# Layer 0's routed experts: slots sorted in one run per array half, weights gathered by indirect loads into six fixed buffers, the shared expert ahead of them

## The chip, the cores and the metric

The kernel runs on one core of a Trainium2 chip. The metric is the device time of one execution in microseconds (us). Before the change, three runs took 3437.78, 3443.05 and 3444.62 us (median 3443.05).

## The reference

A four-layer network on a sequence of 8 x 64 = 512 tokens of width 512 (float32); every layer has a cross attention, a second mixer and a feed-forward, each added to the residual. The change is in the feed-forward of layer 0, a mixture of eight experts of which each token uses two, plus a shared expert that all tokens use:

```python
    def _L0_ffn_ref(x, ln_scale, ln_bias, gate_w, Wg, Wu, Wd, sWg, sWu, sWd):
        ...
        xn = (xf - mu) * jax.lax.rsqrt(var + LN_EPS) * ln_scale + ln_bias
        logits = xn @ gate_w.T
        probs = jax.nn.softmax(logits, axis=-1)
        tk_probs, tk_idx = jax.lax.top_k(probs, TOP_K)
        tk_probs = tk_probs / (jnp.sum(tk_probs, axis=-1, keepdims=True) + EPS)
        ...
        out = _swiglu(xf, sWg, sWu, sWd)
        for e in range(NUM_EXPERTS):
            out = out + w[:, e:e + 1] * _swiglu(xf, Wg[e], Wu[e], Wd[e])
```

with `_swiglu(x, wg, wu, wd) = silu(x @ wg) * (x @ wu) @ wd`. The hidden width of an expert is 1024, so each of its three matrices has 512 x 1024 float32 values, 2 MiB (2.097 MB).

## The kernel before

The kernel is one program for the core's five engines (TensorE, abbreviated PE; VectorE, DVE; ScalarE, ACT; GpSimd, POOL; SyncE, SP), written engine by engine. Each engine runs its own list in order, and semaphores (`wait_ge`, `then_inc`) tie the lists together. A stage ends when all engines have ended their lists for it.

`L0_ffn` first normalises the tokens (`normalise`), then routes. Each expert's tokens are cut into slots of 64 rows; the 1024 token-expert pairs and eight experts need at most 23 slots. Routing runs on VectorE: scores, the two best experts, the rank of each token within its expert (TensorE's `rank`), from that the slot row of each token (`where_to`, ready with the signal `placed`), and the expert of each slot from slot 8 on (`ids`, ready with `ids_ready`). The first slot of expert e is slot e; further slots of crowded experts come behind, from slot 8 on. POOL then scatters the token rows into the table `slot_x` in DRAM (8 indirect transfers, L1764), and reads the slots back by groups (`load`, L1770).

TensorE works on two slots at a time, one per half of its array (64 columns of the 128). Such a group, of which there are 12 (`GROUPS`, the fourth has one slot), runs through: gate and up matmuls (L1863, into four PSUM banks), turning of the next group's tokens (L1836), turning of the hidden rows (L1876), down matmuls (L1888). ACT applies silu and copies results out of PSUM, VectorE multiplies gate and up (L2064). POOL stores the group's output rows into the table `slot_y` (L1781). At the end POOL gathers every token's two rows from `slot_y` (L1786), VectorE adds them weighted (L2082); the last group doesn't go through DRAM but through a matmul with one-hot rows (`hots`, turned at L1895; used at L1901) and an addition (L2087).

The weights come through a ring of eight units of 2 MiB in SBUF, filled by SP in the order of use (`units`): shared up columns 0 to 3, then for each group its gate, up and down matrices; the shared up columns 4 to 7 after the third group (`UP_AFTER`), the shared down matrix after the seventh (`DOWN_AFTER`). The first eight units are sent ahead, during `normalise` (L177): the experts of slots 0 to 7 are known without routing. Each later unit waits for the matmuls that read the unit eight places before it (L1750, L1747); from slot 8 on SP reads the expert's number from `ids`.

The shared expert's up part (`shared_up`, L1827) runs by eight column blocks: the first four during routing, followed by idle matmuls (`run_idle`, L150) until the slots are there, the other four after the third group; its down part (L1911) after the seventh group.

Of the kernel before, what the change touches and what calls it, by code (L numbers as in the profile page):

```python
# [20 lines left out]
LAST_ROWS = SLOT_ROWS - P  # L21
# [1574 lines left out]
def L0_xattn_and_attn(m):  # L1596
# [4 lines left out]
    with m.local(qT=[P, C, N], oT=[P, C, N], w=[P, C, D], bo=[P, D], b=[P, 3, C],  # L1601
# [3 lines left out]
        def clear_slots(pool):  # L1605
            pool.memset(zero[:], 0.0).then_inc(*zeroed.up())
            pool.wait_ge(*zeroed.at(1))
            for p in range(SLOT_ROWS // P):
                pool.dma_start(m.slot_x[p * P:(p + 1) * P, :], zero[:]).then_inc(*filled.up(16))
            pool.dma_start(m.slot_y[LAST_ROWS:SLOT_ROWS, :], zero[:]).then_inc(*filled.up(16))  # L1610

        def slots_cleared(pool):
            pool.wait_ge(*filled.at(SLOT_ROWS // P * 16 + 16))
# [34 lines left out]
def L0_ffn(m):  # L1648
# [9 lines left out]
    s = m.sig  # L1658
    vectors = s("gate_vectors")
    landed = [s(f"unit_landed{r}") for r in range(R)]  # L1660
# [12 lines left out]
    units, read_by = [], []  # L1673
    done = {"Wg": gate_done, "Wu": lift_done, "Wd": down_done}
    halves = [0]
    for p, group in enumerate(GROUPS):
        halves.append(halves[-1] + len(group))
    units.append(("up", 0))
    read_by.append((up_done, 4))
    for p, group in enumerate(GROUPS):  # L1680
        for name in ("Wg", "Wu", "Wd"):
            for slot in group:
                units.append((name, slot))
                read_by.append((done[name], p + 1 if name == "Wd" else halves[p + 1]))
        if p == UP_AFTER:
            units.append(("up", 1))
            read_by.append((up_done, FC))
        if p == DOWN_AFTER:
            units.append(("down", 0))
            read_by.append((shared_done, T))  # L1690
    where = {key: u for u, key in enumerate(units)}
    parts = [2 if name == "up" else 1 for name, _ in units]

    def after(u):
        return 16 * sum(parts[v] for v in range(u % R, u + 1, R))

    with m.local(ring=[P, R, C * F], gw=[P, C, E], gws=[P, 2, C, E], ln=[P, 2, C], before=[P, E, E], place=[P, E]) as \
            (ring, gw, gws, ln, before, place):
        def rows_of(u, k):
            return ring[:, u % R, :].rearrange("p (k f) -> p k f", k=k)  # L1700

        def pairs_of(u):
            name, slot = units[u]
            if name == "up":
                part = ring[:, u % R, :].rearrange("p (two k f) -> p two k f", two=2, k=C)
                cols = slice(HALF * slot, HALF * slot + HALF)
                return [(part[:, i], d[f"L0_ffn_{w}"][E, :, :, cols]) for i, w in enumerate(("Wg", "Wu"))]
            if name == "down":
                return [(rows_of(u, FC), d["L0_ffn_Wd"][E])]
            return [(rows_of(u, FC if name == "Wd" else C), d[f"L0_ffn_{name}"][slot])]  # L1710

        normalise(m, m.y, m.x, 1e-5, dstT=m.yT, ahead=[
            *[(landed[u], *pairs_of(u)) for u in range(1)],
# [3 lines left out]
            *[(landed[u], *pairs_of(u)) for u in range(1, R)]])  # L1717
        vectors_made = vectors.made
        first_landed = [(landed[r].sem, landed[r].made) for r in range(R)]
        with m.local(hs=[P, FC, N], xt=[P, 2, D], xT=[P, 2, C, P], sg=[P, 2, HALF], h=[P, F], hT=[P, FC, P], o=[P, 2, D],  # L1720
                     w=[P, T, E], sc=[P, T, E], sel=[P, T, E], pos=[P, T, E], tmp=[P, T, E], one=[P, T],
                     cmp=[P, T, E, E], eq=[P, T, E, E], tri=[P, P], full=[P, P], nb=[P, 5, E], least=[P, 2, T],
                     share=[P, 2, T], marks=[1, 2 * E], idf=[1, 2 * E], index=[P, P], hots=[P, 2, T, P], hotsT=[P, N],
                     away=[P, 2, T]) as \
                (hs, xt, xT, sg, h, hT, o, w, sc, sel, pos, tmp, one, cmp, eq, tri, full, nb, least, share, marks, idf,
                 index, hots, hotsT, away), \
                m.nc.sbuf_tensor("slot_of_token", [P, 2, T], mybir.dt.uint32) as where_to, \
                m.nc.sbuf_tensor("expert_of_slot", [1, 2 * E], mybir.dt.int32) as ids, \
# [3 lines left out]
            def await_unit(eng, u):  # L1732
                sem, made_before = first_landed[u % R]
                eng.wait_ge(sem, made_before + after(u) - after(u % R))

            @block.sync
            def _(sp):
                for u in range(R, len(units)):
                    name, slot = units[u]
                    signal, n = read_by[u - R]  # L1740
                    sp.wait_ge(*signal.at(n))
                    if name in done and slot >= E:
                        if (name, slot) == ("Wg", E):
                            sp.wait_ge(*ids_ready.at(1))
                        expert = sp.value_load(ids[0:1, slot - E:slot - E + 1], min_val=0, max_val=E)
                        source = d[f"L0_ffn_{name}"][bass.ds(expert, 1)].rearrange("o p k f -> p (o k) f")
                        sp.dma_start(rows_of(u, FC if name == "Wd" else C), source).then_inc(*landed[u % R].up(16))  # L1747
                    else:
                        for dst, source in pairs_of(u):
                            sp.dma_start(dst, source).then_inc(*landed[u % R].up(16))  # L1750

            @block.gpsimd
            def _(pool):
# [13 lines left out]
                pool.wait_ge(*scattered.at(32 * T))  # L1767

                def load(p):
                    pool.dma_start(xt[:, p % 2, :], m.slot_x[p * P:(p + 1) * P, :]).then_inc(*x_landed[p % 2].up(16))  # L1770

                load(0)
                load(1)
                for p in range(len(GROUPS)):
                    if p + 2 <= LAST:
                        pool.wait_ge(*x_turned.at(p + 1))
                        load(p + 2)
                    if p == LAST:
                        break
                    pool.wait_ge(*o_taken.at(p + 1))  # L1780
                    pool.dma_start(m.slot_y[p * P:(p + 1) * P, :], o[:, p % 2, :]).then_inc(*stored[p % 2].up(16))  # L1781
                for i in range(2):
                    pool.wait_ge(*stored[i].at(16 * ((LAST + 1 - i) // 2)))
# [8 lines left out]
            def _(pe):  # L1792
# [25 lines left out]
                def shared_up(n):  # L1818
                    u = where[("up", n // 4)]
                    wb = ring[:, u % R, :].rearrange("p (two k f) -> p two k f", two=2, k=C)  # L1820
                    if n % 4 == 0:
                        await_unit(pe, u)
                    if n >= 2:
                        pe.wait_ge(*hs_ready.at(n - 1))
                    for kind in range(2):
                        for k in range(C):
                            ins = pe.matmul(ps[:, 2 * kind + n % 2, :], wb[:, kind, k, n % 4 * P:(n % 4 + 1) * P],  # L1827
                                            m.yT[:, k, :], start=(k == 0), stop=(k == C - 1))
                    ins.then_inc(*up_done.up())

                def turn_x(p):
                    pe.wait_ge(*x_landed[p % 2].at(16 * (p // 2 + 1)))
# [9 lines left out]
                for n in range(4):  # L1842
                    shared_up(n)
                    if n == 1:
                        rank()
# [2136 lines left out]
```

## Time and profile before

| | |
|---|---|
| three runs | 3437.78, 3443.05, 3444.62 us |
| profiled execution: span from first to last instruction | 3436.7 us |
| profiled execution: time outside the span | not shown by the page; the median of the runs is 6.4 us above the span |
| PE busy | 3113.6 us (91%) |
| DVE, ACT, POOL busy | 1225.3, 710.6, 391.5 us (36, 21, 11%) |
| DMA | 653.75 MB, mean 190 GB/s |
| the stage of the change | about 413 to 838 us of the span |

A busy PE is not PE at its peak; idle time of an engine that isn't the bottleneck costs nothing. A matmul of float32 data shows as two records. Loads are credited to the queue that describes them: the hardware queue (q1) for those issued by SP, the software queue (q0) for those issued by POOL; both use the same 16 DMA engines. A DMA share of 1.00 means that all 16 were busy.

### The profile page before, as it was taken

What the parts mean: (1) busy time and instruction counts of PE and PEld (TensorE: products, weight loads), DVE (VectorE), ACT (ScalarE), POOL (GpSimd) and SP (SyncE); (2) the same over time, 40 slices, a digit from 0 to 9 for tenths busy, and PEclk for the clock granted to TensorE, in tenths of its full rate; (3) what the DMA queues carried; (4) which work ended last, traced back from release to release, by engine and by line L of the source; (5) the groups of instructions that cost most, each with busy time, mean ns of one, the idle gap of its engine ahead of it and who ended that gap; (6) DMA issues with size and microseconds to landing.
All of it is one profiled execution on the core that took longest, in us unless ns stands there. A gap on an engine that the chain in (4) does not pass through costs nothing. (4 is left out here: it accounts for less than half of the span.)

```text
span 3436.7 us, 44844 instructions
## 1 busy us (share of the span) xinstructions
PE 3113.6 (91%) x18245; PEld 1708.9 (50%) x18245; DVE 1225.3 (36%) x2569; ACT 710.6 (21%) x1365; POOL 391.5 (11%) x386
## 2 busy tenths in 40 slices
PE   9998999998999999999899999999999997666666
PEld 6776643434444544444567675446886742111111
DVE  3675520002444569865341223114555220000000
ACT  2443111011333331110112130104442311000000
POOL 4452010001000000001000000005441000000000
PEclk9999999999999999999999999999999999788888
DMA  3112189997111212220641113971103069999998
GB/s 108 46 34 78 74 337 412 419 409 323 74 49 49 77 31 68 98 98 25 236 158 43 52 63 118 421 304 50 37 13 136 29 268 417 420 420 420 420 420 359
DMA packets 104218, 653.75 MB, mean 190 GB/s; under 512 B 20216, under 2 KB 29432, under 8 KB 41208
## 3 DMA queue, kind: packets, MB, share of 16 engines
q1 hardware_dynamic: 99360, 637.67, 46.2%
q0 software_dynamic: 4160, 13.63, 1.0%
q8 instruction: 120, 1.97, 0.2%
q14 instruction: 42, 0.34, 0.0%
q10 hardware_dynamic: 536, 0.14, 0.0%
HBM read 641.89 MB, written 9.50 MB: 190 GB/s over the span
## 5 line engine op out<-in xcount | busy, mean ns | idle before, releaser
L3105 PE MATMUL banks<-ring,h 128*32 128x512 f32 x1024 | 164.9, 750 | 87.0 <-DMA ring<-in_L_ffn_w 62.2
L3088 PE MATMUL banks<-ring,mine 128*32 128x512 f32 x1024 | 165.2, 695 | 54.8 <-DMA ring<-in_L_ffn_w 54.3
L924 PE MATMUL banks<-ring 128*128 128x256 f32 x784 | 179.9, 381 | 0.0
L1863 PE MATMUL banks<-ring,xT 128*64 128x512 f32 x736 | 165.4, 603 | 12.1 <-DMA ring<-in_L_ffn_Wg 6.1
L509 PE MATMUL banks<-normed_features,first 128*128 128x256 f32 x768 | 167.2, 379 | 0.4 <-ACT normed_features L476 0.4
L3216 DVE COPY mine<-mT 128x32 f32<-128x32 f32 x31 | 5.6, 181 | 446.4 <-PE banks L3088 446.4
L924 PEld LDWEIGHTS banks<-ring 128*128 128x128 f32 x784 | 144.5, 190 | 28.7 <-issue 11.4
L509 PEld LDWEIGHTS banks<-normed_features,first 128*128 128x128 f32 x768 | 145.3, 190 | 21.6 <-issue 2.0
L434 POOL TENSOR_TENSOR rstd_pairs<-var_eps_pairs,minus_half 128x4 f32<-128x4 f32 x30 | 30.8, 1028 | 1072.9 <-DVE var_eps_pairs L422 897.5
L3105 PEld LDWEIGHTS banks<-ring,h 128*32 128x32 f32 x1024 | 25.9, 121 | 197.6 <-DMA ring<-in_L_ffn_w 148.5
L1863 PEld LDWEIGHTS banks<-ring,xT 128*64 128x64 f32 x736 | 60.7, 139 | 113.3 <-issue 112.2
L3088 PEld LDWEIGHTS banks<-ring,mine 128*32 128x32 f32 x1024 | 34.5, 117 | 165.1 <-DMA ring<-in_L_ffn_w 112.8
L897 PE MATMUL banks<-big 128*128 128x512 f32 x256 | 115.5, 595 | 0.0
L893 PE MATMUL banks<-big 128*128 128x512 f32 x256 | 113.1, 595 | 1.0 <-ACT big L1067 1.0
L3354 PE MATMUL banks<-big,ring 128*128 128x512 f32 x256 | 111.2, 594 | 0.0
L150 PE MATMUL banks<-identity 128*128 128x128 f32 x740 | 96.4, 290 | 12.7 <-PEq L142 12.7
L150 PEld LDWEIGHTS banks<-identity 128*128 128x128 f32 x740 | 92.2, 204 | 21.1 <-issue 20.8
L1888 PE MATMUL banks<-ring,hT 128*64 128x512 f32 x368 | 89.2, 619 | 14.2 <-DMA ring<-in_L_ffn_Wd 11.7
L2064 DVE TENSOR_TENSOR h<-banks,sg 128x512 f32<-128x512 f32 x23 | 15.9, 692 | 239.4 <-PE banks L1863 214.3
L509 PE MATMUL banks<-normed_features,ring 128*128 128x256 f32 x448 | 97.7, 379 | 0.9 <-DMA bo<-in_L_xattn_bo 0.5
L509 PEld LDWEIGHTS banks<-normed_features,ring 128*128 128x128 f32 x448 | 84.6, 190 | 13.4 <-issue 1.1
L3354 PEld LDWEIGHTS banks<-big,ring 128*128 128x128 f32 x256 | 48.2, 190 | 62.6 <-issue 62.6
(668 smaller groups left out, 5280.7 us busy)
## 6 DMA issues: line engine op xcount, KB each, us to landing
ring<-in_L_ffn_w SPq DMA_DIRECT2D x256, 1024.0 KB, 27.1
ring<-in_L_ffn_Wd SPq DMA_DIRECT2D x24, 2048.0 KB, 21.4
ring<-in_L_ffn_Wg SPq DMA_DIRECT2D x23, 2048.0 KB, 24.7
ring<-in_L_ffn_Wu SPq DMA_DIRECT2D x23, 2048.0 KB, 19.4
wb<-in_L_ffn_W SPq DMA_DIRECT2D x32, 1024.0 KB, 19.3
first<-in_L_ffn_W SPq DMA_DIRECT2D x16, 1024.0 KB, 14.5
second<-in_L_ffn_W SPq DMA_DIRECT2D x12, 1024.0 KB, 18.5
ctxT<-in_ctxT SPq DMA_DIRECT2D x8, 1024.0 KB, 4.9
```

What stands on the lines that cost most here:

```text
L150: pe.matmul(m.ps[:, bank, 0:P], m.ident[:], m.ident[:], start=True, stop=True)
L434: pool.tensor_tensor(m.rstd2[:, 2 * half:2 * half + 2, :].rearrange("p t i -> p (t i)"), m.den2[:, 2 * half:2 * half + 2, :].rearrange("p ...
L509: ins = pe.matmul(m.ps[:, self.banks[q % R], 0:256], w[:, k, mm * P:(mm + 1) * P], m.yT[:, k, 256 * half:256 * half + 256], start=(k == 0) ...
L893: ins = pe.matmul(ps[:, u % 2, :], wkb[:, k, u * P:(u + 1) * P], (extraT if knorm else ctxT[:, par])[:, k, :], start=(k == 0), stop=(k == ...
L897: ins = pe.matmul(ps[:, u % 2, :], ctxT[:, par, k, r * P:(r + 1) * P], wvb[:, k, :], start=(k == 0), stop=(k == C - 1))
L924: ins = pe.matmul(halves(n % 2)[:, r, :], a, x, start=(k == 0), stop=(k == 1))
L1863: ins = pe.matmul(ps[H * side:H * side + H, 2 * kind + half, :], xT[:, p % 2, k, H * own:H * own + H], rows_of(where[(name, slot)], C)[:, ...
L1888: ins = pe.matmul(ps[H * side:H * side + H, 6, :], part, rows_of(where[("Wd", slot)], FC)[:, k, :], start=(k == 0), stop=(k == FC - 1))
L2064: dve.tensor_tensor(h[:, HALF * half:HALF * half + HALF], ps[:, 2 + half, :], sg[:, half, :], ALU.mult)\
L3088: ins = pe.matmul(ps[B4 * q:B4 * q + B4, 0, :], mine[:, e % 2, k, :], w[:, q * 512:(q + 1) * 512], start=(k == 0), stop=(k == C - 1))
L3105: ins = pe.matmul(ps[B4 * q:B4 * q + B4, 2, :], h[:, Q * n + q, :], w[:, q * D:(q + 1) * D], start=(n == 0), stop=(n == Q - 1))
L3354: ins = pe.matmul(bank, self.slot(f, 8)[:, k, :], self.u[:, k, :], start=(k == 0), stop=(k == 7))
```

## The change

The slots are numbered in one sorted run: all slots of expert 0, then of expert 1, and so on, at least one for each. The first 12 (0 to 11) belong to one array half (side 0), the next 11 to the other (side 1); group p works on slot p of each side, and the last group has one slot. Since no slot's expert is known ahead of routing, VectorE makes for each slot and each partition the row of the weight tables at which that partition's 16 KB begin (`from_row`), and POOL loads each slot's three matrices by an indirect transfer of 128 such rows. Each of the three names has one buffer per side, six in all; a buffer is loaded again when the matmuls that read it are done. The slots' token rows and outputs are moved by SP instead, as two halves of 64 rows. The shared expert's up part runs whole before the experts, then its down part; its matrices are sent ahead during `normalise`, the up part into the memory that later holds the two down buffers. The 30 idle matmuls after the shared up part are gone. TensorE does the down matmuls of group p - 1 after the gate and up matmuls of group p.

The core of the diff:

```diff
-    SLOTS = 2 * N // H + E - 1
-    GROUPS = [(0, 1), (2, 3), (4, 5), (6,)] + [(slot, slot + 1) for slot in range(7, SLOTS, 2)]
-    LAST = len(GROUPS) - 1
-    UP_AFTER, DOWN_AFTER, OWN_AFTER = 2, 6, 4
-    R = 8
+    GROUPS = SLOT_ROWS // P
+    LAST, SLOTS = GROUPS - 1, 2 * GROUPS
+    NAMES = ("Wg", "Wu", "Wd")
+    sides = lambda p: (0, 1) if p < LAST else (0,)
...
+        swup = ring[:, 4:6, :].rearrange("p two (k f) -> p two k f", k=C)
+        unit = lambda name, side: ring[:, 2 * NAMES.index(name) + side, :]
...
             @block.sync
-                for u in range(R, len(units)):
...
+                sp.wait_ge(*scattered.at(32 * T))
+                def load(p):
+                    for side in range(2):
+                        sp.dma_start(xt[H * side:H * side + H, p % 2, :], slot_rows(m.slot_x, p, side))\
+                          .then_inc(*x_landed[p % 2].up(16))
+                load(0)
+                load(1)
+                for p in range(GROUPS):
+                    if p + 2 <= LAST:
+                        sp.wait_ge(*x_turned.at(p + 1))
+                        load(p + 2)
+                    if p:
+                        sp.wait_ge(*o_taken.at(p))
+                        for side in range(2):
+                            sp.dma_start(slot_rows(m.slot_y, p - 1, side), o[H * side:H * side + H, (p - 1) % 2, :])\
+                              .then_inc(*stored[(p - 1) % 2].up(16))
...
             @block.gpsimd          # after the eight scatters
+                def fetch(name, p):
+                    for side in sides(p):
+                        pool.indirect_dma_start(
+                            out=unit(name, side), out_offset=None, in_=d[f"L0_ffn_{name}"].rearrange("e p k f -> (e p) (k f)"),
+                            in_offset=bass.IndirectOffsetOnAxis(ap=from_row[:, side, p:p + 1], axis=0)).then_inc(*landed[name, side].up(16))
+                pool.wait_ge(*ids_ready.at(1))
+                fetch("Wg", 0)
+                fetch("Wu", 0)
+                pool.wait_ge(*up_done.at(FC))
+                fetch("Wd", 0)
+                for p in range(GROUPS):
+                    if p < LAST:
+                        pool.wait_ge(*gate_done.at(halves[p + 1]))
+                        fetch("Wg", p + 1)
+                        pool.wait_ge(*lift_done.at(halves[p + 1]))
+                        fetch("Wu", p + 1)
+                    if p:
+                        pool.wait_ge(*down_done.at(p))
+                        fetch("Wd", p)
...
             @block.tensor
+                run_idle(m, pe, 7, 6)
+                pe.wait_ge(*made.at(2))
+                gate()
+                for n in range(FC):
+                    shared_up(n)
+                    if n == 1:
+                        rank()
+                pe.wait_ge(*hs_ready.at(FC))
+                pe.wait_ge(shared_down_landed.sem, shared_down_before + 16)
+                for t in range(T):
+                    if t == T - 1:
+                        turn_x(0)
+                    shared_down(t)
+                pe.wait_ge(*own_ready.at(1))
+                ...                                       # own rows turned, as before
+                for p in range(GROUPS):
+                    pe.wait_ge(*x_taken.at(p + 1))
+                    lift(p, 0)                            # gate: waits for landed["Wg", side]
+                    lift(p, 1)                            # up: waits for landed["Wu", side]
+                    if p:
+                        down(p - 1)                       # waits for landed["Wd", side]
+                    if p < LAST:
+                        turn_x(p + 1)
+                    turn_h(p)
+                down(LAST)
...
             @block.vector
-                step(dve.tensor_scalar(nb[:, 0, :], nb[:, 0, :], -1.0, 0.0, ALU.add, ALU.max))
+                step(dve.tensor_scalar(nb[:, 0, :], nb[:, 0, :], 1.0, None, ALU.max))
...
+                step(dve.tensor_reduce(flat, sorted_by, X, ALU.add))
+                step(dve.tensor_scalar(flat, flat, E - 1.0, None, ALU.min))
+                dve.tensor_scalar(from_row[:].rearrange("p a b -> p (a b)"), flat, float(P), line[:], ALU.mult, ALU.add)\
+                   .then_inc(*ids_ready.up())
...
+                step(dve.tensor_scalar(off[:], index[:], H - 0.5, -4096.0, ALU.is_gt, ALU.mult))
+                step(dve.tensor_tensor(index[:], index[:], off[:], ALU.add))
```

In layer 0's attention, POOL clears the last group's two half blocks of `slot_y` with two transfers instead of one (`clear_slots`).

## Rows read from the trace of the kernel before

**Rows 1.** The page's 40 equal slices of the span, in tenths and GB/s:
```profile
PE   9998999998999999999899999999999997666666
...
GB/s 108 46 34 78 74 337 412 419 409 323 74 49 49 77 31 68 98 98 25 236 158 43 52 63 118 421 304 50 37 13 136 29 268 417 420 420 420 420 420 359
```

**Rows 2.** Windows: us, busy time by engine, PEclk, DMA share, GB/s:
```profile
core 0: us, PE busy (x) PEld busy (x) DVE busy (x) ACT busy (x) POOL busy (x), PEclk, DMA share, GB/s
548.00:578.00 30.00, 28.50 (x70) 12.24 (x68) 2.76 (x4) 2.98 (x5) 1.07 (x2) 1.00 1.01 427
...
413.00:838.00 425.00, 391.32 (x1673) 175.16 (x1674) 63.66 (x156) 42.22 (x72) 30.60 (x44) 0.96 0.92 380
```

**Rows 3.** Groups of PE's instructions, 413 to 838 us: busy, mean ns | idle before:
```profile
L1863 PE MATMUL banks<-ring,xT 128*64 128x512 f32 x736 | 165.4, 603 | 12.1 <-DMA ring<-in_L_ffn_Wg 6.1 <-DMA ring<-in_L_ffn_Wu 3.7 <-DVE hs L1962 1.5
L1888 PE MATMUL banks<-ring,hT 128*64 128x512 f32 x368 | 89.2, 619 | 14.2 <-DMA ring<-in_L_ffn_Wd 11.7 <-ACT hT L1941 2.4
L1827 PE MATMUL banks<-normed_features,ring 128*128 128x512 f32 x128 | 59.9, 630 | 0.0
```

**Rows 4.** DMA view of 720 to 820 us; queues: packets, MB, share of 16 engines:
```profile
DMA packets 3531, 42.42 MB, mean 424 GB/s; under 512 B 463, under 2 KB 463, under 8 KB 1101
...
q1 hardware_dynamic: 2737, 39.75, 93.9%
q0 software_dynamic: 790, 2.61, 6.5%
```

**Rows 5.** DMA view of 2850 to 3400 us, the last layer's weights:
```profile
DMA packets 31897, 230.65 MB, mean 419 GB/s; under 512 B 3765, under 2 KB 3765, under 8 KB 3765
```

**Rows 6.** Timeline of SP's issues: start, us; last one sent ahead, next one:
```profile
421.88 0.65 SPq L177 DMA_DIRECT2D ring<-in_L_ffn_Wg  x1
467.93 0.33 SPq L1750 DMA_DIRECT2D ring<-in_L_ffn_Wg  x1
```

**Rows 7.** Timeline of 455 to 560 us, all engines [idle before <-releaser]:
```profile
456.32 1.09 POOL L1764 DMA_INDIRECT slot_inputs<-normed_tokens,slot_of_token  x1 [27.50 <-DVE slot_of_token L2036]
...
456.75 0.16 DVE L2043 CAST expert_of_slot<-idf 1x16 int32<-1x16 f32 x1
...
465.33 0.96 POOL L1764 DMA_INDIRECT slot_inputs<-normed_tokens,slot_of_token  x1 [0.30 <-issue]
...
467.73 6.86 PE L150 MATMUL banks<-identity 128*128 128x128 f32 x60
...
468.33 1.18 POOL L1770 DMA_DIRECT2D xt<-slot_inputs  x2 [2.04 <-DMA slot_inputs<-normed_tokens,slot_of_token]
...
478.03 13.95 PE L1863 MATMUL banks<-ring,xT 128*64 128x512 f32 x64 [0.75 <-ACT xT L1925]
```

**Rows 8.** Timeline of PE, 548 to 578 us, shared up columns 4 to 7:
```profile
548.63 27.73 PE L1827 MATMUL banks<-normed_features,ring 128*128 128x512 f32 x64
577.87 0.65 PE L1863 MATMUL banks<-ring,xT 128*64 128x512 f32 x2 [1.50 <-DVE hs L1962]
```

**Rows 9.** Timeline of PE: own rows, shared down, one group of experts:
```profile
616.90 2.05 PE L1895 MATMUL banks<-identity,hots 128*128 128x128 f32 x16
...
668.01 27.73 PE L1911 MATMUL banks<-ring,hs 128*128 128x512 f32 x64
695.68 13.95 PE L1863 MATMUL banks<-ring,xT 128*64 128x512 f32 x64
709.56 0.66 PE L1836 MATMUL banks<-identity,xt 128*128 128x128 f32 x4
710.05 1.10 PE L1876 MATMUL banks<-identity,h 128*128 128x128 f32 x8
711.48 7.09 PE L1888 MATMUL banks<-ring,hT 128*64 128x512 f32 x32 [0.33 <-ACT hT L1941]
```

**Rows 10.** DMA issues in 470 to 480 us: count, KB each, us to landing:
```profile
xt<-slot_inputs POOLq DMA_DIRECT2D x1, 256.0 KB, 3.2
```

**Rows 11.** Timeline of the stage's end, first and last instruction:
```profile
822.22 9.61 PE L1888 MATMUL banks<-ring,hT 128*64 128x512 f32 x32 [3.58 <-DMA ring<-in_L_ffn_Wd]
...
836.25 0.69 DVE L2087 TENSOR_TENSOR x_tokens<-banks,x_tokens 128x512 f32<-128x512 f32 x1 [0.17 <-PE banks L1901]
```

More of the change, by code:

```diff
@@ L1671, in L0_ffn @@
     down_done, o_taken, back = s("slot_down"), s("slot_o_taken"), [m.fresh(f"rows_back{t}") for t in range(T)]
[L1673 to L1710, printed above, removed]
+    with m.local(ring=[P, 6, C * F], swdown=[P, FC, D], gw=[P, C, E], gws=[P, 2, C, E], ln=[P, 2, C],
+                 before=[P, E, E], place=[P, E]) as (ring, swdown, gw, gws, ln, before, place):
+        swup = ring[:, 4:6, :].rearrange("p two (k f) -> p two k f", k=C)
+        unit = lambda name, side: ring[:, 2 * NAMES.index(name) + side, :]
+        weights = lambda name, side: unit(name, side).rearrange("p (k f) -> p k f", k=FC if name == "Wd" else C)
+        slot_rows = lambda table, p, side: table[(GROUPS * side + p) * H:(GROUPS * side + p + 1) * H, :]
+        shared_before = [sig.made for sig in shared_landed]
+        shared_down_before = shared_down_landed.made
@@ new lines, in lift @@
+                def lift(p, kind):
+                    name, signal = (("Wg", gate_done), ("Wu", lift_done))[kind]
+                    for side in sides(p):
+                        pe.wait_ge(*landed[name, side].at(16 * (p + 1)))
+                    for half in range(len(sides(p))):
+                        if p == 0:
+                            pe.wait_ge(*shared_added.at(2 * kind + half + 1))
+                        elif kind == 0 and half == 0:
+                            pe.wait_ge(*h_ready.at(halves[p]))
+                        for k in range(C):
+                            for side in range(2):
+                                own, part = (side, half) if p < LAST else (0, side)
+                                ins = pe.matmul(ps[H * side:H * side + H, 2 * kind + half, :],
+                                                xT[:, p % 2, k, H * own:H * own + H],
+                                                weights(name, own)[:, k, HALF * part:HALF * part + HALF],
+                                                start=(k == 0), stop=(k == C - 1))
+                        ins.then_inc(*signal.up())
@@ L1871, in _, with turn_h @@
+                def turn_h(p):
+                    for half in range(len(sides(p))):
                         pe.wait_ge(*h_ready.at(halves[p] + half + 1))
-                        if p == OWN_AFTER + 1 and half == 0:
+                        if p == 0 and half == 0:
                             pe.wait_ge(*own_taken.at(1))
@@ L1877, in _, with down @@
                         ins.then_inc(*turned.up())
-                    for slot in group:
-                        await_unit(pe, where[("Wd", slot)])
+                def down(p):
+                    for side in sides(p):
+                        pe.wait_ge(*landed["Wd", side].at(16 * (p + 1)))
                     if p:
@@ L1882, in _ @@
                     for k in range(FC):
-                        if k % 4 == 0:
+                        if k % 4 == 0 and (k == 0 or p < LAST):
                             pe.wait_ge(*(dve_took if k else act_took).at(p + 1))
-                        for side, slot in enumerate(group):
-                            part = hT[:, k, H * side:H * side + H] if len(group) == 2 else \
+                        for side in sides(p):
+                            part = hT[:, k, H * side:H * side + H] if p < LAST else \
```

222 lines of the change are left out of this document (72 added, 150 removed).

## The prediction

> **What bounds the kernel now.** I read the page's busy slices first, to see which stretch the change sits in. The routed feed-forward of layer 0 is the run of high GB/s in slices 5 to 10 (337 to 419 GB/s), and in the same slices PE stays at 8 or 9 tenths [rows 1]: TensorE and the DMA engines are both nearly full. The table of windows gives the stage its size: from 413 to 838 us PE is busy 391.3 of 425 us while 380 GB/s flow, and in a stretch where PE runs shared matmuls the DMA share is 1.01 at 427 GB/s [rows 2]. Third, the groups of instructions: the idle time ahead of the expert matmuls is 12.1 us (gate and up) and 14.2 us (down), most of it waits for weights [rows 3]. Those about 26 us are all that PE loses to loads; the stage is balanced, and 60 us of shared up matmuls [rows 3] and 27.7 us of shared down [rows 9], half of the former and all of the latter between the experts, give the queue time to catch up. Fourth, the DMA view: in 720 to 820 us the transfers move at a mean of 424 GB/s. Dividing bytes by occupied engine time (share x 16 engines x 100 us), the hardware queue's 16 KB rows go at 423 GB/s and the software queue's 2 KB rows at 2.61 MB/6.5 us = 401 GB/s [rows 4]. The last layer's weight stream, another long one, runs at 419 GB/s [rows 5].
>
> **Bytes.** Before: 69 slot loads of 2.097 MB plus the shared expert's 6.29 MB. After: exactly the same. 23 slots, three matrices each, every one loaded again. What changes is when they may move, and the queue that describes them.
>
> **The front.** Before, eight ring units (16.8 MB) had been sent by 422.5 us, seven of them for experts known without routing; the next issue is at 467.9 [rows 6]. After, only the shared expert's 6.29 MB goes ahead (done by about 430 at 424 GB/s), and all expert loads wait for the routing. The expert numbers are ready at about 457 us, but on POOL eight scatters stand first: 456.3 to 466.3 us, landed by 468.3 [rows 7]. So the fetches of group 0 start near 466.5, at 0.96 + 0.30 = 1.26 us of POOL each, and its gate and up weights (8.4 MB, 20 us) land near 489. Its down weights share memory with the shared up weights and wait for the last shared up matmul.
>
> PE's front grows. Columns 0 to 3 of the shared up part end at 467.7, and 6.9 us of idle matmuls follow [rows 7]; these go. Columns 4 to 7 come here instead: 27.7 us [rows 8], to 495.4. The wait for the last activated column, 1.5 us [rows 8], was met once in mid-stage and now stands here, to 497. Then the shared down part 27.7 us, turning group 0's tokens 0.7, and the own-row turn 2.1 [rows 9]: 527.5 us. Before, experts began at 478.0 [rows 7]. Group 0's weights have long landed (down weights near 508), so the changed DVE operations of the router cost nothing here: they are a handful of the kind of the cast at 456.75 (0.16 us [rows 7]; the wider ones perhaps twice that), beside the scatters on POOL and 70 us of shared matmuls on PE; if that cover went they would cost about 1 us. Nor does the second small clear of the slot table in layer 0's attention: one more POOL issue of about 0.6 us [rows 7], long before. Both are taken as 0 (bounds -1 to +1).
>
> PE does not lose by this as such: 88 us of shared work moves from mid-stage to the front. The DMA engines lose: group 1's gate weights have nowhere to go until group 0's gate matmuls free their buffers at 527.5 + 7.0 = 534.5 (half of the 13.95 us for gate and up [rows 9]). The queue is empty from about 430 to 466, 489 to 496, and 507 to 537 us, about 73 us, against 44 us of slack in the whole stage before (380 of 424 GB/s [rows 2, 4] over 425 us).
>
> **The steady part.** Per group PE needs 13.95 + 0.66 + 1.10 + 7.09 = 22.8 us [rows 9]. The loads need 12.58 MB plus 0.52 MB of slot rows in and out, 13.1/0.424 = 30.9 us. So the loads set the pace. Does single buffering break the stream? Three names take turns, 10.3 us each. Gate weights land at 0, gate runs 0 to 7 and frees them; up weights land at 10.3 and the previous group's down weights at 20.6; the next gate weights, issued near 8, get their turn at 20.6. Each load is queued 12 us ahead of its turn, and 5 us ahead even if each set of matmuls took 14 us instead of 7. The queue stays full. That takes issue and first byte as about 3 us, as an idle 256 KB load lands in 3.2 us [rows 10].
>
> Slot rows and outputs move from POOL's queue to SP, as two halves each. SP has nothing else to issue; it may hold a load of rows behind the store of an output, but rows are fetched a group (31 us) before they are turned, and the buffer of an output is wanted two groups later. Taken as 0; without that lead a late half would cost one landing, 3.2 us, per group, 38 us in all. For POOL the six fetches of a group cost 6 x 1.26 = 7.6 of 31 us.
>
> Sum: after 537 us come 10 groups x 12.58 + 6.29 = 132.1 MB of weights, ten loads of slot rows 2.6 MB and the stores 2.7 MB: 137.4 MB, less the last down load 2.1 MB = 135.3 MB. At 424 GB/s [rows 4] this is 319 us, to 856, landed 857.5. I take 424 and not 401, since 95% of these bytes are the 16 KB rows of the former; 401 stays as a bound (+18 us), 427 [rows 2] as the other (-2).
>
> **The tail.** The last group's down weights use a buffer that frees only after the down matmuls of the group before: 857.5 + 7.1 = 864.6, issue 1.3, 4.9 us of bytes and 2.6 us of landing: 873.4. Before, the same weights were in flight ahead, and from their landing to the end of the stage took 822.2 to 836.9 = 14.7 us [rows 11]; the same here (now 16 unpaired matmul records in place of 32 paired ones, about 7 us either way at full clock): 888.1. The gathers of slot rows end earlier: output copied 865.2, stored about 869, eight issues of 1.26 us to 879, landed 881.
>
> **Sum.** 888.1 - 836.9 = +51 us on the stage, and the next stage starts from its end. The profiled span 3436.7 becomes 3488. The runs are 3437.8 to 3444.6 and the page gives no time of the profiled execution but its span, so I add 51 to the median, 6.4 us above that span: 3443 + 51 = 3494 us (+1.5%).
>
> **A rule against the trace.** The scatters show that the software queue's transfers overlap: eight of 256 KB, issued 1.27 us apart, had all landed 3 us after the last issue began [rows 7]. The Trainium skill ("DMA: Bandwidth & Descriptors", Bandwidth) gives GpSimd-issued loads 341 GB/s at 1 MB and 425 GB/s at 16 MB, one at a time. This trace agrees in so far as overlapping transfers don't each pay a landing; by the lower figure 135.3 MB would take an estimated 397 us, +78 on the forecast.
>
> The lead of 12 us says that three names in turn do the work of a second buffer. The Trainium skill ("Trainium Kernel Development and Optimization", Best Practices) advises a second buffer so that loads and compute overlap, and each name has only one here; no stage of this trace is built so, and the rival "loads and matmuls take turns" is what the rule would make of it.
>
> **The rivals.**
> - *Slow queue.* Rows described by GpSimd move under 401 GB/s. For: its 2 KB rows are the slower of the two now [rows 4]. Against: 16 KB rows have an eighth of the pieces. At 350 GB/s: 135.3/0.35 - 319 = +68 more, 3562. Chance 0.12.
> - *POOL is the bound.* If issuing costs by bytes and not by rows, 1.26 us per 256 KB [rows 7] is 10.1 us per load; 66 loads after group 0 take 667 us instead of 319: about 3840. Against: a load has 128 rows like a scatter. Chance 0.05.
> - *Loads and matmuls take turns.* If a load didn't queue behind the others, a group would be 30.9 + 22.8 us: eleven times 22.8 more, 250 us, about 3745. Chance 0.03.
> - *Not slower: PE sets the pace.* PE alone would need 527.5 + 11.5 x 22.8 + 15 = 805, 32 us under 837: 3411 at the best. It decides at the rate where the stream ends 51 us sooner: 135.3 MB/268 us = 505 GB/s. Against it: the long windows show 419 to 427 [rows 2, 4, 5]. Chance 0.06, half of it within the noise.
>
> **How the numbers follow.** The forecast (rates 401 to 427, front and tail within 15 us) has 0.74: 3494, own range 3477 to 3520. With the slow queue down to about 345 GB/s the range is 3474 to 3566, which leaves out the two dearer rivals, the other side and the worst of the slow queue. A measurement of this kernel tells about 0.2% (7 us) from no change. Faster 0.03, same 0.03, slower 0.94.
>
> **What would show it.** Right: the first expert matmul near 527 us; GB/s near zero about 510 to 535; then groups about 31 us apart, PE waiting about 2.7 us before each of gate, up and down, with a weight load as releaser; an 8 us hole in the DMA before the last down matmuls; the stage ending near 888. Wrong: groups 23 us apart (PE sets the pace); DMA share under 0.9 with PE waiting (turns, or POOL busy most of the time); or share 1.0 with GB/s under 400 (slow queue).

## The result, and the profile after

| | before | after |
|---|---|---|
| median of 4 runs | 3442.67 us (3437.78 to 3444.62) | 3515.94 us (3514.06 to 3520.60) |
| ratio | 1 | 1.0218, 95% interval 1.0205 to 1.0231 |
| span of the profiled execution | 3436.7 us | 3518.9 us |
| start of the next stage (first statistics on DVE) | 837.25 us | 906.51 us |

The change makes the kernel 73 us slower; the forecast was 51. The stage itself ends 69.3 us later, before and after:
```profile
837.25 1.42 DVE L409 BATCH_NORM_STATS2 stats<-x_tokens 128x6 f32<-128x512 f32 x2 [0.30 <-PEq L142]
...
906.51 1.42 DVE L409 BATCH_NORM_STATS2 stats<-x_tokens 128x6 f32<-128x512 f32 x2 [0.30 <-PEq L142]
```

The page's slices, PE and GB/s, answer to [rows 1]:
```profile
PE   9999998777899999999999999999999997666666
...
GB/s 106 45 33 76 86 176 370 412 410 347 173 50 52 21 78 57 108 25 120 135 142 109 45 109 91 293 388 87 36 24 47 113 239 359 420 420 420 420 420 372
```
Counted from 0, PE falls to 7 tenths in slices 7 to 9, where it had 8 or 9. Slices 5 and 6 lost bytes (176 and 370 GB/s in place of 337 and 412), and slices 9 and 10 pay them back (347 and 173 in place of 323 and 74).

Windows of the kernel after (columns as in [rows 2]):
```profile
core 0: us, PE busy (x) PEld busy (x) DVE busy (x) ACT busy (x) POOL busy (x), PEclk, DMA share, GB/s
430.00:466.00 36.00, 36.00 (x110) 19.30 (x111) 12.98 (x64) 3.90 (x6) 8.89 (x10) 0.92 0.25 101
...
506.00:537.00 31.00, 31.00 (x119) 13.50 (x119) 2.76 (x4) 2.39 (x4) 1.88 (x2) 1.00 0.17 57
...
413.00:905.00 492.00, 396.78 (x1608) 168.48 (x1606) 62.30 (x154) 42.00 (x72) 83.42 (x90) 0.93 0.82 328
...
545.00:850.00 305.00, 241.67 (x1056) 93.49 (x1058) 20.05 (x29) 26.99 (x47) 52.43 (x56) 0.93 1.00 408
```
PE is busy about as long as before (396.8 against 391.3 us [rows 2]), but over 492 us in place of 425. From 545 to 850 us every DMA engine is busy all the time and 408 GB/s flow; from 430 to 466 and 506 to 537 little does (101 and 57 GB/s).

The groups of PE's instructions, 413 to 906 us, answer to [rows 3]:
```profile
L1834 PE MATMUL banks<-ring,xT 128*64 128x512 f32 x736 | 180.7, 648 | 51.3 <-DMA ring<-in_L_ffn_Wu,weight_row_of_slot 34.9 <-DMA ring<-in_L_ffn_Wg,weight_row_of_slot 16.4
L1861 PE MATMUL banks<-ring,hT 128*64 128x512 f32 x368 | 89.5, 617 | 33.5 <-issue 25.1 <-DMA ring<-in_L_ffn_Wd,weight_row_of_slot 8.4
```
The idle time ahead of the expert matmuls grew from 26.3 to 84.8 us, 58.5 more, in the same 1104 matmuls. (For 25.1 us ahead of the down matmuls the profile names no releaser; they are put down to Wd, since they are gone in e6 below, where most loads are left out.)

The start, and one group, by the timelines of POOL and PE; answers to [rows 7, 9]:
```profile
464.66 1.00 POOL L1743 DMA_INDIRECT ring<-in_L_ffn_Wg,weight_row_of_slot  x1 [0.30 <-issue]
...
523.80 13.95 PE L1834 MATMUL banks<-ring,xT 128*64 128x512 f32 x64
...
545.78 9.90 PE L1834 MATMUL banks<-ring,xT 128*64 128x512 f32 x32 [6.51 <-DMA ring<-in_L_ffn_Wg,weight_row_of_slot]
...
666.72 7.09 PE L1834 MATMUL banks<-ring,xT 128*64 128x512 f32 x32 [1.42 <-DMA ring<-in_L_ffn_Wg,weight_row_of_slot]
678.10 8.60 PE L1834 MATMUL banks<-ring,xT 128*64 128x512 f32 x32 [4.29 <-DMA ring<-in_L_ffn_Wu,weight_row_of_slot]
688.75 7.09 PE L1861 MATMUL banks<-ring,hT 128*64 128x512 f32 x32 [2.05 <-issue]
...
698.70 3.65 PE L1834 MATMUL banks<-ring,xT 128*64 128x512 f32 x16 [1.40 <-DMA ring<-in_L_ffn_Wg,weight_row_of_slot]
```
Gate matmuls start 32.0 us apart (666.72 to 698.70), with a wait ahead of each of the three names.

The end of the stage; answers to [rows 11]:
```profile
868.87 8.79 PE L1861 MATMUL banks<-ring,hT 128*64 128x512 f32 x32 [7.31 <-issue]
...
877.94 0.94 POOL L1743 DMA_INDIRECT ring<-in_L_ffn_Wd,weight_row_of_slot  x1 [22.40 <-PE banks L1861]
...
878.32 1.08 SPq L1722 DMA_DIRECT2D slot_outputs<-o  x2
...
886.68 8.42 PE L1861 MATMUL banks<-ring,hT 128*64 128x512 f32 x16 [8.43 <-DMA ring<-in_L_ffn_Wd,weight_row_of_slot]
...
887.06 0.95 POOL L1765 DMA_INDIRECT hs<-slot_outputs,slot_of_token  x1 [8.19 <-DMA slot_outputs<-o]
...
903.72 2.48 DVE L2067 TENSOR_TENSOR x_tokens<-banks,x_tokens 128x512 f32<-128x512 f32 x4
```
The last load does start only after the down matmuls before it (877.94), as forecast. But the store of group 10's outputs, issued 0.4 us behind that load, lands with it (8.19 us of POOL's waiting), so the eight gathers begin at 887 and they, not the last matmuls, set the end.

The DMA view of 560 to 860 us; answers to [rows 4]:
```profile
GB/s 428 428 416 376 428 426 424 360 426 424 430 353 431 424 427 371 412 428 429 389 392 426 428 404 383 428 424 424 372 426 422 425 376 420 422 426 428 428 428 299
DMA packets 10934, 123.09 MB, mean 410 GB/s; under 512 B 1455, under 2 KB 1455, under 8 KB 3702
...
q0 software_dynamic: 8118, 118.33, 95.9%
```
Each slice is 7.5 us. Most stand at 420 to 430; once per group, every fourth slice, one falls to 353 to 390. The mean is lower because of a dip that comes with each group, not because the queue is slow throughout.

### The profile page after: what moved, and what is told of

Same layout as the page of the kernel before. It is cut to its first block and busy times, and to the rows that moved or that the text cites. A ratio compares the mean times of both kernels' runs of the same rounds, so it can differ in the third digit from the quotient of the medians.

```text
span 3518.9 us, 44513 instructions
## 1 busy us (share of the span) xinstructions
PE 3133.2 (89%) x18185; PEld 1714.6 (49%) x18185; DVE 1225.2 (35%) x2570; ACT 710.1 (20%) x1365; POOL 444.8 (13%) x433
## 2 busy tenths in 40 slices
DMA packets 106072, 653.73 MB, mean 186 GB/s; under 512 B 20600, under 2 KB 29816, under 8 KB 43064
## 3 DMA queue, kind: packets, MB, share of 16 engines
q0 software_dynamic: 12272, 152.31, 10.8%
## 5 line engine op out<-in xcount | busy, mean ns | idle before, releaser
L1834 PE MATMUL banks<-ring,xT 128*64 128x512 f32 x736 | 180.7, 648 | 51.3 <-DMA ring<-in_L_ffn_Wu,weight_row_of_slot 34.9
L3068 PE MATMUL banks<-ring,mine 128*32 128x512 f32 x1024 | 159.5, 680 | 61.6 <-DMA ring<-in_L_ffn_w 61.1
L924 PEld LDWEIGHTS banks<-ring 128*128 128x128 f32 x784 | 144.6, 190 | 28.7 <-issue 11.4
L1861 PE MATMUL banks<-ring,hT 128*64 128x512 f32 x368 | 89.5, 617 | 33.5 <-issue 25.1
L2053 DVE TENSOR_TENSOR h<-banks,sg 128x512 f32<-128x512 f32 x23 | 15.9, 691 | 218.4 <-PE banks L1834 218.4
L3156 POOL TENSOR_TENSOR normed_tokens<-fold,keb 128x512 f32<-128x512 f32 x9 | 9.4, 1042 | 587.9 <-PE banks L3103 548.2
## 6 DMA issues: line engine op xcount, KB each, us to landing
wb<-in_L_ffn_W SPq DMA_DIRECT2D x32, 1024.0 KB, 19.5
```

Source lines behind the costliest of these rows:

```text
L924: ins = pe.matmul(halves(n % 2)[:, r, :], a, x, start=(k == 0), stop=(k == 1))
L1834: ins = pe.matmul(ps[H * side:H * side + H, 2 * kind + half, :], xT[:, p % 2, k, H * own:H * own + H], weights(name, own)[:, k, HALF * par ...
L1861: ins = pe.matmul(ps[H * side:H * side + H, 6, :], part, weights("Wd", side)[:, k, :], start=(k == 0), stop=(k == FC - 1))
L2053: dve.tensor_tensor(h[:, HALF * half:HALF * half + HALF], ps[:, 2 + half, :], sg[:, half, :], ALU.mult)\
L3068: ins = pe.matmul(ps[B4 * q:B4 * q + B4, 0, :], mine[:, e % 2, k, :], w[:, q * 512:(q + 1) * 512], start=(k == 0), stop=(k == C - 1))
```

## Experiments

Ten runs: e0 to e3 on one chip beside the kernel before (3438.76 us), e4 to e7 beside 3437.39, e8 and e9 beside 3443.04. "Stage" is the start of the next stage against 837.25 us before, each read from one execution; "first" is the start of the first expert matmul in it. Groups of the changed kernel are about 31.9 us apart.

| run | median us | ratio to before, 95% | stage | first, us | 560 to 820 us |
|---|---|---|---|---|---|
| e0 changed kernel again | 3522.63 | 1.0245 (1.0231 to 1.0260) | +75.0 | 528.63 | 406 GB/s |
| e1 shared down between | 3491.42 | 1.0156 (1.0141 to 1.0171) | +47.0 | 498.31 | 410 |
| e2 whole rows | 3503.80 | 1.0190 (1.0174 to 1.0205) | +60.9 | 528.81 | 423 |
| e3 last down early | 3512.90 | 1.0216 (1.0195 to 1.0237) | +67.4 | 527.72 | 411 |
| e4 all three | 3477.91 | 1.0111 (1.0091 to 1.0131) | +28.7 | 496.74 | 421 |
| e5 pairs in halves | 3518.29 | 1.0227 (1.0209 to 1.0245) | +71.9 | 528.51 | 410 |
| e6 skip repeats | 3419.26 | 0.9939 (0.9922 to 0.9956) | -26.6 | 527.71 | pace set by PE |
| e7 skip, shared down between | 3411.74 | 0.9916 (0.9899 to 0.9932) | -37.2 | 495.94 | pace set by PE |
| e8 cut by columns | 3514.57 | 1.0208 (1.0195 to 1.0222) | +61.1 | 524.07 | 425 |
| e9 cut in quarters | 3519.64 | 1.0227 (1.0213 to 1.0242) | +69.2 | 523.67 | 410 |

**e0, the yardstick.** 

> The changed kernel again, as the base of the runs beside it. Both theories expect about 73 us over the kernel before (3442.7 to 3515.9 us, ratio 1.0213).

The experts start at 528.63 us in place of 523.80, with a granted clock of 0.86 in 430 to 466 us (0.92 in the first execution): about 5 us of the front differ from one execution to the next, and such a difference in "first" is part of "stage" too.

**e1, does the empty queue of the front cost the time?** The shared down part goes back between groups 0 to 3.
```diff
-                for t in range(T):
-                    if t == T - 1:
-                        turn_x(0)
-                    shared_down(t)
+                turn_x(0)
...
                     turn_h(p)
+                    if p < T:
+                        shared_down(p)
```


> The shared expert's down part leaves the front: one of its four token tiles (6.9 us) after each of the first four groups, in a bank of the up matmuls. Theory 'the loads set the pace, and the queue lies empty in the front': experts begin 27.7 us sooner, near 496 us, so the stream of loads starts 28 us sooner and ends 28 us sooner; the moved matmuls fit into the PE waits (8 us a group). Stage and total fall by 25 to 28 us against the changed kernel (about 3490). Rival 'PE sets the pace once the experts run': the same matmuls only change places, total within 5 us of the changed kernel.

-31.2 us against e0. The first expert matmul of e1 on PE's timeline:
```profile
498.31 13.95 PE L1834 MATMUL banks<-ring,xT 128*64 128x512 f32 x64
```
It is 30.3 us ahead of e0's, with the same matmuls and bytes in all, and the end of the stage moves by 28.0. PE's 27.7 us of shared down now lie beside the stream; in front of it they were a hole in the DMA queue. The theory of the front holds, and the rival (PE's order doesn't matter) falls.

**e2, why 408 and not 424 GB/s?** Slots in pairs, so that a group's slot rows and outputs are one 128-row transfer each, on the same queue.
```diff
-                    for side in range(2):
-                        sp.dma_start(xt[H * side:H * side + H, p % 2, :], slot_rows(m.slot_x, p, side))\
-                          .then_inc(*x_landed[p % 2].up(16))
+                    sp.dma_start(xt[:, p % 2, :], slot_rows(m.slot_x, p)).then_inc(*x_landed[p % 2].up(16))
```


> Slots dealt in pairs (slots 2p and 2p + 1 to group p), so that a group's token rows and its outputs are one block of 128 rows each and move in one transfer instead of two of 64. Weights, loads and matmuls as in the changed kernel. Theory 'the half transfers slow the weight packets': the dip from 425 to 350 GB/s that comes once a group (about 6 us long, while the 16 KB packets take 710 to 770 instead of 616 ns) goes, the period of a group falls from 31.9 to 30.9 us, total 9 to 12 us under the changed kernel. Rival 'the software queue itself delivers less': period stays 31.9 us, total within 4 us of the changed kernel.

-18.8 us, more than expected. The DMA view of e2, 560 to 820 us:
```profile
DMA packets 9567, 110.08 MB, mean 423 GB/s; under 512 B 1056, under 2 KB 1056, under 8 KB 3104
...
q0 software_dynamic: 7254, 105.75, 96.1%
```
The rate of [rows 4] is back, with 96% of the engines' time on the software queue: rows described by GpSimd are not slower. The tail gained too: in e2 the one store, issued after the last load like the two of the changed kernel, landed 2.8 us after its issue began. PE and the tail of e2:
```profile
528.81 13.95 PE L1830 MATMUL banks<-ring,xT 128*64 128x512 f32 x64
...
863.64 9.11 PE L1857 MATMUL banks<-ring,hT 128*64 128x512 f32 x32 [7.63 <-issue]
...
873.02 0.94 POOL L1739 DMA_INDIRECT ring<-in_L_ffn_Wd,weight_row_of_slot  x1 [23.05 <-PE banks L1857]
...
873.41 0.32 SPq L1719 DMA_DIRECT2D slot_outputs<-o  x1
...
876.21 0.95 POOL L1761 DMA_INDIRECT hs<-slot_outputs,slot_of_token  x1 [2.26 <-DMA slot_outputs<-o]
```
Its issue ended at 873.73, before POOL's at 873.96; the second store of the changed kernel ended its issue at 879.40, after POOL's at 878.88. The DMA queues of the changed kernel from 881.5 to 884 us, and of e2 from 872 to 874.9 us (packets, MB, share):
```profile
q0 software_dynamic: 60, 0.98, 91.7%
q1 hardware_dynamic: 59, 0.10, 10.3%
...
q1 hardware_dynamic: 110, 0.23, 22.0%
```
In the changed kernel the stores' packets (q1) move side by side with the load's (q0); in e2 they go first. That the order of the two issues decides this is read from these times; no run changed the order alone.

**e5, e8 and e9: the halves, or the order of the slots?** e5 keeps e2's pairs and cuts each transfer into two of 64 rows, e9 into four of 32; e8 cuts it into two of 128 half rows.
The two ends of a transfer in e5, with those of e8 and of e9 in their place (`half(side)` is 256 of the 512 columns):
```diff
-    xt[H * side:H * side + H, p % 2, :], table[(2 * p + side) * H:(2 * p + side + 1) * H, :]
+    xt[:, p % 2, half(side)], table[p * P:(p + 1) * P, half(side)]
...
+    xt[32 * part:32 * part + 32, p % 2, :], table[p * P + 32 * part:p * P + 32 * part + 32, :]
```


> The slots in pairs as with whole rows, but every 128-row transfer cut into two of 64 rows again. If the cut into halves is what slows the weights' packets, this stands where the changed kernel stands: within 4 us of 3522, about 407 GB/s from 560 to 840 us, the dip of some 6 us per group back, groups about 31.9 us apart. If the order of the slots is what helped (both sides of a group reading the same expert's rows), it stands where whole rows stood: about 3504, 424 GB/s, groups about 30 us apart.

> Slots in pairs; each slot transfer cut in two as in the kernel with pairs in halves, but by columns: two transfers of 128 rows of 1 KB instead of two of 64 rows of 2 KB. If it is the 64 partitions that slow the weights' packets, this stands with whole rows: about 3504 us, 420 GB/s or more from 560 to 820 us, no dip. If it is the number of transfers, it stands with the halves: about 3518 to 3522, about 410 GB/s, a dip per group.

> Slots in pairs, each slot transfer cut in four of 32 rows. If covering fewer partitions at a time is what costs, the loss against whole rows at least doubles: under 400 GB/s from 560 to 820 us, groups near 33.5 us, about 3535 us or more. If the loss is the same for any cut into rows, it stands with the halves, about 3518 to 3522 us and 410 GB/s.

The same line of the DMA view, 560 to 820 us, of e5:
```profile
DMA packets 9585, 106.62 MB, mean 410 GB/s; under 512 B 1285, under 2 KB 1285, under 8 KB 3333
```
of e8:
```profile
GB/s 426 431 421 428 417 432 424 426 426 426 429 422 428 426 421 435 427 423 419 426 427 429 421 425 421 429 427 425 427 426 426 424 427 424 426 427 426 425 418 429
DMA packets 12012, 110.62 MB, mean 425 GB/s; under 512 B 1328, under 2 KB 5522, under 8 KB 5522
```
and of e9:
```profile
DMA packets 10101, 106.51 MB, mean 410 GB/s; under 512 B 1808, under 2 KB 1808, under 8 KB 3856
```
Twice as many transfers over all 128 partitions cost the stream nothing (425, no dip); 64 partitions cost 13 to 15 GB/s (e5 against e2 and e8), and 32 cost 15, not twice as much: e5's order theory and e9's first theory fall. The trace's packets say the same: from 600 to 850 us 16% of e5's 16 KB weight packets took over 650 ns, 0.2% of e2's and 0.5% of e8's, at a median of 614 ns in e5 and e2. So narrow transfers hold up the wide stream beside them.

e8's median is 71.5 us above its kernel before, e2's 65.0, although both stages end alike in the profiled executions (+61.1, +60.9). But e8's profiled execution, the fastest of its five, had its first expert matmul 4.7 us earlier than e2's. From there to the end of the stage e8 took 374.3 us and e2 369.3, and the 5 us lie in the tail: POOL waits for e8's two stores as it did in the changed kernel, though they are 128 partitions wide (the second issue ended at 869.00, the load's at 868.74).
```profile
524.07 13.95 PE L1835 MATMUL banks<-ring,xT 128*64 128x512 f32 x64
...
878.93 0.95 POOL L1766 DMA_INDIRECT hs<-slot_outputs,slot_of_token  x1 [10.19 <-DMA slot_outputs<-o]
```

The Trainium skill ("SBUF — State Buffer", Door 1: The DMA port swizzle) says that partitions 0 to 63 reach no more of the memory's 16 DMA ports than 0 to 31 do, 8 of them. By that rule halves and quarters would load the same ports and cost the same, and column cuts nothing, and the three rates agree; no run here shows the ports themselves. The Trainium skill ("DMA: Bandwidth & Descriptors", Rules for kernel authors) also advises one 128-partition transfer over two to disjoint halves; the runs agree, and show that the price falls on the other traffic (425 to 410 GB/s).

**e3, the last down load.** It goes into a gate buffer that has been free since the last gate matmuls, and so ahead of the down matmuls of group 10.
```diff
+                        if p < LAST:
+                            pool.wait_ge(*down_done.at(p))
+                            fetch("Wd", p)
+                        if p == LAST - 1:
+                            fetch_last_down()
```


> The last group's down matrix goes into the gate buffer of side 1, which the last group doesn't use, right behind the loads of the group before; it no longer waits for that group's down matmuls. Theory 'the tail waits for that load': the 8.4 us wait ahead of the last down matmuls goes, but then the gathers of slot rows end the stage: the last store is issued near 878 us as before, lands about 5 us sooner with no load ahead of it, and the stage ends 5 to 9 us sooner. Rival 'the gathers alone end the stage, at their own pace': under 3 us gained. Rival 'only the down load counts': 13 us gained.

-9.7 us, though its runs reach to e0's (3506.64 to 3521.65); the stage gains 7.6, of which 0.9 is an earlier first expert matmul. The end of e3's stage:
```profile
882.75 7.05 PE L1873 MATMUL banks<-ring,hT 128*64 128x512 f32 x16 [0.78 <-ACT hT L1944]
...
882.05 1.08 SPq L1724 DMA_DIRECT2D slot_outputs<-o  x2
...
885.18 0.95 POOL L1775 DMA_INDIRECT hs<-slot_outputs,slot_of_token  x1 [26.18 <-DMA slot_outputs<-o]
```
The 8.8 us wait ahead of the last down matmuls (in e0) is gone, and with no load in flight the stores land 3.1 us after their issue began in place of 8.7 (878.32 to 887.06). Now the eight gathers alone hold the end.

**e4, do the three add?** The edits of e1, e2 and e3 in one kernel. 

> The shared down part between the groups, whole 128-row slot transfers and the early last down load in one kernel. If the three costs are separate stretches of the same stage (empty queue in the front, a slower stream, a late last load), they add: 3522.6 - 31.2 - 18.8 - 8 to 10 = 3461 to 3466 us; the stream at about 424 GB/s from about 505 us, no wait over 2 us before the last down matmuls, the next stage starting near 858 to 862 us. If two of them are the same time seen twice (the late store and the late last load end on the same gathers), the sum falls short by about 8: 3470 to 3476. Either way it stays some 20 us above the kernel before, since the front still costs about 20 us of empty queue.

By the end of the stage, nearly: -46.3 us against e0, where the three alone gave -28.0, -14.2 and -7.6, sum -49.8. By the median they fall short, 12 to 17 us over what was expected, since medians also count what comes after the stage: taking the stage's difference from the median's leaves 8.9 us in e0, 5.7, 4.1 and 6.7 in e1, e2 and e3, and 11.8 in e4. No run takes apart the 28.7 us that are left; the first expert matmul still starts 18.7 us later than before (496.74 against 478.03 [rows 7]).

**e6, does the pace follow the bytes?** A slot whose expert is the same as the slot's before it on its side gets row numbers beyond the table, and the load skips such rows.
```diff
-    in_offset=bass.IndirectOffsetOnAxis(ap=from_row[:, side, p:p + 1], axis=0)).then_inc(*landed[name, side].up(16))
+    in_offset=bass.IndirectOffsetOnAxis(ap=from_row[:, side, p:p + 1], axis=0),
+    bounds_check=(E + 1) * P - 1, oob_is_err=False).then_inc(*landed[name, side].up(16))
...
+                repeat = cmp[:, 0:2, 0:2, :].rearrange("p a b c -> p a (b c)")[:, :, 0:GROUPS - 1]
+                step(dve.tensor_tensor(repeat, eid[:, :, 1:GROUPS], eid[:, :, 0:GROUPS - 1], ALU.is_equal))
...
+                step(dve.scalar_tensor_tensor(eid[:, :, 1:GROUPS], repeat, 4096.0, eid[:, :, 1:GROUPS], ALU.mult, ALU.add))
...
```


> A slot whose expert is that of the slot before it on its side fetches nothing: its row numbers lie beyond the table, and such rows are skipped. At most 9 runs of one expert are left, 27 loads or 56.6 MB in place of 69 and 144.7 MB. If the loads set the pace, PE sets it now: groups 22.8 us apart except where the expert changes on both sides at once, the stage ends near 527 + 11.5 x 22.8 + 20 = 810 us (up to 825 with waits at the changes) in place of 906 to 912, and the run takes 3415 to 3435, under the kernel before. Rival: the pace is set by issuing and by the chain of waits from one name to the next, not by bytes; then skipping saves only the bytes' share beyond it and groups stay above 28 us, 3480 or more.

It beats both kernels, the one before by 0.6%, and the stage ends at 810.7 us as forecast. PE's groups of e6, 413 to 884 us, and the starts of three groups:
```profile
L1835 PE MATMUL banks<-ring,xT 128*64 128x512 f32 x736 | 163.2, 602 | 3.7 <-DMA ring<-in_L_ffn_Wg,weight_row_of_slot 3.7
L1862 PE MATMUL banks<-ring,hT 128*64 128x512 f32 x368 | 86.1, 597 | 4.9 <-DMA ring<-in_L_ffn_Wd,weight_row_of_slot 4.9
```
```profile
546.92 16.60 PE L1835 MATMUL banks<-ring,xT 128*64 128x512 f32 x64 [3.73 <-DMA ring<-in_L_ffn_Wg,weight_row_of_slot]
...
571.78 13.95 PE L1835 MATMUL banks<-ring,xT 128*64 128x512 f32 x64
...
593.99 13.95 PE L1835 MATMUL banks<-ring,xT 128*64 128x512 f32 x64
```
Groups are 22.2 us apart with the same issues by POOL and the same waits: it was the bytes. The software queue's total falls from 152.31 to 64.25 MB, 42 of 69 loads.

**e7, the best version.** e6 with e1's edit. 

> Skipped repeats and the shared down part between the groups. With PE setting the pace it doesn't matter where PE does the shared down part: within 6 us of the kernel that only skips repeats, the experts starting about 28 us earlier and the first four groups 6.9 us further apart each. If loads still set the pace in the first groups, this one gains up to the 27.7 us that the move gave without skipping.

3411.74 us, 0.8% under the kernel before; against e6 it gains 7.5 us, and its stage ends 10.6 us sooner, more than the 6 expected. PE's groups of e7:
```profile
L1835 PE MATMUL banks<-ring,xT 128*64 128x512 f32 x736 | 160.6, 594 | 0.0
L1862 PE MATMUL banks<-ring,hT 128*64 128x512 f32 x368 | 87.5, 601 | 5.0 <-DMA ring<-in_L_ffn_Wd,weight_row_of_slot 5.0
```
Group 1's wait (3.7 us) and its matmuls at a lower granted clock (0.84 from 546.9 to 563.5 us, 16.60 us in place of 13.95) are gone, 6.4 us; the other 4 are an earlier front (shared up ends that much earlier), which the edit doesn't touch.

## Why the prediction was right, and where it was off

The sign and the mechanism were right, and the stage was mis-sized by 18 us (906.2 against 888.1).

- **Front.** Forecast 527.5, measured 523.8 and 528.6: right. The queue was nearly empty in the two long holes that it named (DMA share 0.25 and 0.17); in the short one, 488 to 497 us, it was half busy (0.57). e1 gives 28 us of the stage back for filling one hole.
- **The steady part.** That the loads set the pace held: share 1.00, groups 32 us apart, waits before each name, and e6 turns the pace into PE's by taking bytes away. The rate was the mis-sized term: 135.3 MB at 408 in place of 424 GB/s take 331.6 us, +12.6. The step that failed is "Slot rows and outputs move from POOL's queue to SP, as two halves each ... Taken as 0": it looked at when the halves arrive, not at what they do to the stream. The bound of 401 covered it, for a wrong reason (the software queue's 2 KB rows, which the trace of before has as packets of 4096 B). From the first expert matmul to group 10's down matmuls it took 345.1 us, 15.1 more than forecast. e2, without the halves, took 334.8 for the same stretch, so by that run the halves are worth 10.3 of the 15.1 (11.0 against e0). About 2 more lie at the end of the stream, where the queue wasn't full as forecast: group 10's down loads were issued only at 853.36, behind the down matmuls before them, and the last group has one load each for gate and up. Windows of the kernel after:
```profile
850.00:855.00 5.00, 5.00 (x32) 2.45 (x30) 0.42 (x1) 1.67 (x3) 1.34 (x2) 1.00 0.75 308
855.00:860.00 5.00, 5.00 (x26) 1.68 (x24) 0.27 (x1) 0.60 (x1) 0.54 (x1) 1.00 0.97 350
```
- **The last load.** Right: 17.8 us from one down matmul to the next against 15.9, the difference being down matmuls of 8.79 us.
- **The gathers.** "Stored about 869 ... landed 881" failed. The store landed 8.7 us after its issue began, not about 4, because the last load was ahead of it; the end came 19.5 us after the last weights in place of 14.7. With -3.7 for the front, +15.1, +1.9 and +4.8 make the 18.
- **After the stage.** "The next stage starts from its end" was right, but the rest of the kernel took 6 to 13 us longer in the profiled execution of each of these eleven, also where the stage ended early (by the medians, less the stage, 4 to 12). All of the rest, before (columns as in [rows 2]):
```profile
837.25:3436.70 2599.45, 2330.38 (x13039) 1237.06 (x13039) 920.09 (x1919) 518.80 (x981) 220.90 (x213) 0.96 0.45 180
```
and in e7:
```profile
800.03:3409.20 2609.17, 2344.19 (x13039) 1247.94 (x13039) 919.34 (x1919) 518.38 (x981) 220.93 (x213) 0.95 0.45 179
```
The same matmuls keep PE busy 13.8 us longer, at a mean granted clock of 0.95 in place of 0.96. Why stays open.
- **The rivals.** *Slow queue* fell: 425 GB/s in e8 with 96% on it. Of the two figures of the Trainium skill ("DMA: Bandwidth & Descriptors", Bandwidth) weighed in the prediction, 341 and 425 GB/s, the trace bears out the higher. *POOL is the bound* fell: a 2.1 MB load costs POOL 0.94 to 1.00 us. *Loads and matmuls take turns* fell: one buffer per name kept the share at 1.00. *PE sets the pace* fell for this kernel; e7 is what it looks like, at 800.0 us with the same PE work.
- **Readings.** Counted from 0, the slices of before that show the stage are 5 to 9, with 323 to 419 GB/s; slice 10 has 74 [rows 1]. And 3494 with +18 for the rate and +15 for front and tail gives an own range up to 3527, not 3520. Nothing above rests on either.

## What to carry to other kernels

When compute and loads are both near their limit, a load that can't be issued early can cost nearly its full time even if TensorE stays busy (in e1 the experts start 30 us sooner and the stage ends 28 us sooner): look for stretches in which the DMA share is near zero, and put work that needs no new weights beside the stream. Keep small side transfers 128 partitions wide, since narrow ones slowed the stream beside them, and let an indirect load skip rows that are in place already. At the end of a stream, ask which small store shares its last microseconds with a big load.

## What the runs showed of the hardware

- An indirect load of 128 rows of 16 KB costs POOL what a scatter of 2 KB rows costs: 0.94 to 1.00 us against 0.96 [rows 7].
- A skipped row is not free of a packet: e6 has 5376 more packets under 512 B than the changed kernel (25976 against 20600), 42 loads of 128 rows; POOL's issue stays at 0.99 us.
